# A third slot of prefix counts and 16 unread products a round in the edge sort of a graph network kernel

## The chip, the cores and the metric

The kernel runs on one core of a Trainium2 chip. The metric is the device time of one execution in microseconds (us), the median of several runs. Engines: TensorE (PE; its weight loads are PEld), VectorE (DVE), ScalarE (ACT), GpSimd (POOL) and SyncE (SP), each with its own in-order instruction stream; they meet by semaphores.

## What is computed

Four graph-network blocks run on one graph of 3125 nodes (48 features) and 100000 edges. Only the first step matters here: before any block can run, the edges are sorted on the chip. The reference, cut to what uses that order:

```
src, dst = edge_index[0], edge_index[1]
gate = silu(edge_attr @ F1W + F1b) @ F2W + F2b           # per edge, 48 wide
msg  = gate * h[dst] * (cw * mj)[:, None]
agg  = segment_sum(msg, src, num_segments=N)             # and softmaxes by src, by dst
```

Segment sums become products with 0/1 matrices if each record of an edge lies in the block of its source (25 blocks of 128 nodes) and the window of its destination (37 windows). So stage "bucket" gives every edge a rank among the edges of its block and window, computes the place from it, and scatters a 92-word record (attributes, gate, weights, source, destination) there in DRAM.

## The kernel before

The edges stand as 782 tiles of 128, and a set is SET = 16 tiles: NS = 49 sets, one for each round x of the stage. TensorE's and VectorE's loops run on to x = 55 and 56 to drain. A record travels through the rounds: `hh` (one-hot rows of window and block) for set x, prefix counts for x, same-cell counts for x - 1, ranks for x - 2, overflow for x - 4 and x - 5, gates for x - 6, places and records for x - 7. The order of the work on each engine is written out by hand; there is no planner.

TensorE, in round x, for each group g = 0 to 3 of four tiles (loop from line 403):

- `turn_hot(x, g)` (line 329): four transposes of `hh` into bank 0. It waits for `s_hot` and for ScalarE's copy of the group before.
- `cross(x, g)` (337, 340): accumulates, for all 17 prefixes of the set, the counts of window by block in partitions 0 to 36 of bank 1. At g = 0 it starts with the last prefix of the set before, read from `pre`, and waits for `s_pre`; at g = 3 it increments `s_cross`.
- `same(x - 1, g)` (350, 353): one 512-column product and four of 128 columns into bank 3.
- at g = 0 and 2 `mix(u)` (311), at g = 1 and 3 `gate(u)` (318), fp32, for the gates of eight tiles.
- at g = 1 `colds` (383, 384) and `spills` (371 to 375).
- after g = 3 `ahead(x - 2)` (361): 16 products of `hT` with `pre` into bank 2, `s_ahead`.

ScalarE copies the transposes to `hT` (440), turns the same-cell counts into `match` (447), and applies silu (433). VectorE, in round x: `one_hot(x + 1)`, `spill_ranks`, `places`, `before(x - 1)` (520: clips bank 1 into a slot of `pre`), two calls of `record` (509, 513: gate and words of eight tiles into `rec`), `pairs` (525), `ranks` (531 to 542). `before(s)` waits for `s_cross` and, as `pre` has two slots, for `ahead(s - 2)`:

```
dve.wait_ge(s_cross, s + 1)
if s >= 2:
    dve.wait_ge(s_ahead, s - 1)
```

GpSimd scatters: sixteen indirect DMAs a round (line 299), one for each tile, each four after a wait for `s_pos` and `s_rec`. The stage ends when they have landed. SyncE loads attributes; ahead of them it fills the lists in DRAM with empty records, and GpSimd waits for that before its first scatter.

Of the kernel before, what the change touches and what calls it, by code (L numbers as in the profile page):

```python
# [11 lines left out]
BF16 = mybir.dt.bfloat16  # L12
# [6 lines left out]
P = 128  # L19
N, E, H, RBF, LAYERS, G = 3125, 100000, 48, 40, 4, 32  # L20
NB = -(-N // P)
# [9 lines left out]
NW = len(WIN)  # L31
# [67 lines left out]
def bc(ap, n):  # L99

    return ap.unsqueeze(2).to_broadcast([ap.shape[0], ap.shape[1], n])
# [7 lines left out]
def along(ap, n):  # L109

    return ap.unsqueeze(1).to_broadcast([ap.shape[0], n, ap.shape[1]])
# [48 lines left out]
def bucket(nc, c, ps, m, a, w, given, list1, list2, wins, ncold, feats, nodes, embp, z, adapt, mult, logm, table0,  # L160
# [13 lines left out]
    SET = 16  # L174
# [4 lines left out]
    S1 = SET + 1  # L179
    HR, TR, MR, SR, LR = 5, 4, 4, 4, 10  # L180
# [2 lines left out]
    GATE, RECORD = 6, 7  # L183

    NAMES, TABLES = 3, NS + 2
    pad, pad2 = m.sb("pad", [P, 10, REC]), m.sb("pad2", [P, NW, 3])
    R = pad.shape[1]
    TIMES = HOT // P // R
# [5 lines left out]
    ge = m.sb("bk_ge", [P, SET, KT], BF16)  # L194
    hT = m.sb("bk_hT", [NW + NB, TR, SET * P], BF16)
    match = m.sb("bk_match", [P, MR, SET * P], BF16)
    pre = m.sb("bk_pre", [NW, 2, S1, NB], BF16)

    spill = m.sb("bk_spill", [P, SR, NB, SET], BF16)
    along_s = m.sb("bk_along", [P, SR, NB, SET], BF16)  # L200
# [8 lines left out]
    tri4 = m.sb("bk_tri4", [P, 4, P], BF16)  # L209
# [26 lines left out]
    with stage(nc, "bucket", *names, *[f"attr{k}" for k in range(4)], *[f"landed{k}" for k in range(RG)],  # L236
# [68 lines left out]
        @block.tensor  # L305
        def _(pe):
            def mix(u):
                pe.wait_ge(s_attr[u % 4], 16 * (u // 4 + 1))
                if u:
                    pe.wait_ge(s_silu, u)  # L310
                pe.matmul(ps[0:2 * H, 6, :], w["F1"][:], attrT[:, u % 4, :], start=True, stop=True).then_inc(s_mixed, 1)

            def gate(u):
                pe.wait_ge(s_silu, u + 1)
                if u >= 2:
                    pe.wait_ge(s_rec, 2 * (u - 1))
                for j in range(4):
                    ins = pe.matmul(ps[:, 5 + 2 * (u % 2), 2 * H * j:2 * H * j + 2 * H], hid[:, u % 2, P * j:P * j + P],  # L318
                                    w["F2"][:], start=True, stop=True)
                ins.then_inc(s_gated, 1)  # L320

            def turn_hot(s, g):
                x = 4 * s + g
                if g == 0:
                    pe.wait_ge(s_hot, s + 1)
                if x:
                    pe.wait_ge(s_flipped, x)
                for j in range(4):
                    ins = pe.transpose(flip[0:NW + NB, P * j:P * j + P], hh[:, s % HR, 4 * g + j, :], c["identb"][:])
                ins.then_inc(s_flip, 1)  # L330

            def cross(s, g):

                bank = ps[0:NW, 1, :]
                if g == 0:
                    pe.wait_ge(s_pre, s + 1)
                    pe.matmul(bank[:, 0:NB * S1], c["identb"][0:NW, 0:NW], along(pre[:, (s + 1) % 2, SET, :], S1), start=True,
                              stop=False)
                for t in range(4 * g, 4 * g + 4):
                    ins = pe.matmul(bank[:, NB * (t + 1):NB * S1], hh[:, s % HR, t, 0:NW], along(hh[:, s % HR, t, NW:], SET - t),  # L340
                                    start=False, stop=(t == SET - 1))
                if g == 3:
                    ins.then_inc(s_cross, 1)

            def same(s, g):
                x = 4 * s + g
                pe.wait_ge(s_flipped, x + 1)
                if x:
                    pe.wait_ge(s_match, x)
                pe.matmul(ps[:, 3, :], c["identb"][:], tri4[:].rearrange("p j e -> p (j e)"), start=True, stop=False)  # L350
                for j in range(4):
                    one = hT[:, s % TR, P * (4 * g + j):P * (4 * g + j) + P]
                    ins = pe.matmul(ps[:, 3, P * j:P * j + P], one, one, start=False, stop=(j == 3))
                ins.then_inc(s_same, 1)

            def ahead(s):
                pe.wait_ge(s_pre, s + 2)
                if s:
                    pe.wait_ge(s_rank, s)
                for t in range(SET):  # L360
                    ins = pe.matmul(ps[:, 2, NB * t:NB * t + NB], hT[0:NW, s % TR, P * t:P * t + P], pre[:, s % 2, t, :],  # L361
                                    start=True, stop=True)
                ins.then_inc(s_ahead, 1)

            def spills(s):
                pe.wait_ge(s_spill, s + 1)
                pe.wait_ge(s_srank, s + 1)
                if s > PLACE - SPILL - 1:
                    pe.wait_ge(s_pos, s - (PLACE - SPILL - 1))
                one, sums = spill[:, s % SR], along_s[:, s % SR]  # L370
                pe.matmul(ps[:, 4, 0:SET * NB], c["identb"][:], bc(carry_s[:], SET), start=True, stop=False)
                pe.matmul(ps[:, 4, SET * NB:S1 * NB], c["identb"][:], carry_s[:], start=False, stop=False)
                pe.matmul(ps[:, 4, 0:SET * NB], low[:], one.rearrange("p b t -> p (b t)"), start=False, stop=False)
                pe.matmul(ps[:, 4, 0:SET * NB], c["onesb"][:], sums.rearrange("p b t -> p (b t)"), start=False, stop=False)
                pe.matmul(ps[:, 4, SET * NB:S1 * NB], c["onesb"][:], sums[:, :, SET - 1], start=False, stop=True
                          ).then_inc(s_spilt, 1)

            def colds(s):
                pe.wait_ge(s_cold, s + 1)
                if s:  # L380
                    pe.wait_ge(s_pos, s)
                one = overb[:, s % LR, :]
                pe.matmul(ps[:, 4, 448:448 + SET], c["tri"][:], one, start=True, stop=True)
                pe.matmul(ps[:, 4, 480:480 + SET], c["onesb"][:], one, start=True, stop=True).then_inc(s_coldsum, 1)

            def turn_type(q):
                pe.wait_ge(s_emb, 16 * NB)
                if q:
                    pe.wait_ge(s_turned, q)
                for j, b in enumerate(by_four[q]):  # L390
                    ins = pe.transpose(ps[0:G, 5, P * j:P * j + P], embn[:, b, :], c["ident"][:])
                ins.then_inc(s_embT, 1)

            def adapted(q):
                pe.wait_ge(s_turned, q + 1)
                if q:
                    pe.wait_ge(s_named, q)
                for j, b in enumerate(by_four[q]):
                    ins = pe.matmul(ps[:, 7, G * j:G * j + G], embT[:, q % 2, P * j:P * j + P], adapt, start=True, stop=True)
                ins.then_inc(s_adapted, 1)  # L400
            pe.wait_ge(s_made, 4)
            pe.wait_ge(s_given, 16 * len(given))
            for x in range(NS + PLACE):
                for g in range(4):
                    if x < NS:
                        turn_hot(x, g)
                        cross(x, g)
                    if 0 <= x - 1 < NS:
                        same(x - 1, g)
                    if 0 <= 4 * (x - NAMES) + g < NQ:  # L410
                        turn_type(4 * (x - NAMES) + g)
                    if 0 < 4 * (x - NAMES) + g <= NQ:
                        adapted(4 * (x - NAMES) + g - 1)
                    if 0 <= x - GATE < NS:
                        u = 2 * (x - GATE) + g // 2
                        if g % 2 == 0:
                            mix(u)
                        else:
                            gate(u)
                    if g == 1 and 0 <= x - COLDS < NS:  # L420
                        colds(x - COLDS)
                    if g == 1 and 0 <= x - SPILL < NS:
                        spills(x - SPILL)
                if 0 <= x - AHEAD < NS:
                    ahead(x - AHEAD)
# [64 lines left out]
        def _(dve):  # L490
# [24 lines left out]

            def before(s):
                dve.wait_ge(s_cross, s + 1)
                if s >= 2:
                    dve.wait_ge(s_ahead, s - 1)
                dve.tensor_scalar(pre[:, s % 2].rearrange("p t b -> p (t b)"), ps[0:NW, 1, 0:NB * S1], 255.0, None, ALU.min  # L520
                                  ).then_inc(s_pre, 1)

            def pairs(s):
# [3062 lines left out]
```

## Time and profile before

| | us |
|---|---|
| median of 3 runs | 6147.38 (6138.8 to 6162.79) |
| span of the profiled execution | 6172.7 |
| TensorE busy, loads beside it | 4389.3 (71%) |
| VectorE busy | 3821.1 (62%) |
| GpSimd busy | 2684.3 (43%) |
| ScalarE busy | 2247.1 (36%) |
| line 299, 782 scatters of GpSimd | 790.6 busy, 529.6 idle before them |
| line 447, ScalarE's match | 134.7 busy, 408.2 idle before it |
| line 520, VectorE's `before` | 29.1 busy, 407.6 idle before it |

How to read it: the page gives shares over the whole span, but only the stage up to about 1370 us, where the last scatter stands, is touched. The idle time that stands before a line says who sits and waits; what ends that idle time is read from the waits and from the timeline of a single round. A matmul row shows when TensorE took the product and a modelled end; when others learn of the end is seen in the start of the row that waited. TensorE's granted clock is 1.0 (2.4 GHz) or 0.5 (1.2 GHz) at any time, and a mean over a stretch lies between.

### The profile page before, as it was taken

The numbers are of one execution on the slowest core, as the hardware profiler recorded it, in microseconds if no ns is written. First come the engines' busy times: TensorE is split into PE (matmuls) and PEld (weight loads), VectorE is DVE, ScalarE is ACT, GpSimd is POOL, SyncE is SP. The second block draws the span as 40 slices with busy tenths as digits, with TensorE's granted clock in tenths as the row PEclk, the third lists the DMA queues.
The fourth block names the chain that finished last, engine by engine and source line by source line (L and its number), as shares of the span: only waits on it lengthen the run. The fifth ranks groups of instructions, "written<-read, shape, count | busy, mean of one in ns | idle before, by whom it ended". The sixth has DMA issues, their size and how long they took to land. (4 is left out here: it accounts for less than half of the span.)

```text
span 6172.7 us, 186442 instructions
## 1 busy us (share of the span) xinstructions
PE 4389.3 (71%) x79347; PEld 3648.8 (59%) x79432; DVE 3821.1 (62%) x7925; ACT 2247.1 (36%) x7746; POOL 2684.3 (43%) x2702
## 2 busy tenths in 40 slices
PE   6676677725666479857985899489837765678887
PEld 3343344414555468846884788478835653677777
DVE  6555555538999767756774677477748335645244
ACT  3222222205666435543553455345520333300320
POOL 2666666666666346624662566256620340000000
PEclk7555555557999789968996999699959788788987
DMA  9222222227777344414331434144324626000000
GB/s 330 53 57 58 56 56 56 59 53 173 199 200 200 100 154 154 150 36 164 146 144 40 160 144 148 53 154 152 130 37 103 215 86 205 3 9 3 5 3 10
DMA packets 488183, 656.79 MB, mean 106 GB/s; under 512 B 316480, under 2 KB 370372, under 8 KB 484117
## 3 DMA queue, kind: packets, MB, share of 16 engines
q1 hardware_dynamic: 450965, 595.00, 30.7%
q0 software_dynamic: 33856, 48.44, 3.2%
q8 instruction: 644, 10.55, 0.7%
q14 instruction: 222, 1.82, 0.1%
q10 hardware_dynamic: 2496, 0.98, 0.1%
HBM read 464.16 MB, written 180.09 MB: 104 GB/s over the span
## 5 line engine op out<-in xcount | busy, mean ns | idle before, releaser
L299 POOL DMA_INDIRECT edges<-sb_bk_rec,sb_bk_pos x782 | 790.6, 1011 | 529.6 <-issue 224.1
L1681 ACT ACTIVATE sb_at_val<-banks,sb_at_prob 128x49 f32<-128x49 f32 x3800 | 773.5, 325 | 519.8 <-PE banks L1621 505.3
L1720 DVE TENSOR_REDUCE sb_at_tops<-banks 128x1 f32<-128x512 f32 x1000 | 626.0, 659 | 326.4 <-PE banks L1601 304.4
L1577 PE MATMUL banks<-sb_near,sb_at_hotT_d 128*128 128x49 bf16 x11100 | 618.8, 185 | 132.0 <-DMA sb_at_hotT_d<-rows_dst_t 65.5
L1535 POOL TENSOR_TENSOR sb_at_key<-sb_at_key,sb_at_attr 128x400 f32<-128x400 f32 (+1 forms) x400 | 371.0, 928 | 714.4 <-ACT sb_at_key L1665 622.1
L1577 PEld LDWEIGHTS banks<-sb_near,sb_at_hotT_d 128*128 128x128 fp8e4 x11100 | 567.1, 97 | 137.3 <-issue 70.7
L1579 PE MATMUL banks<-sb_queryp,sb_at_hotT_s 128*128 128x49 bf16 x11400 | 634.9, 186 | 16.4 <-issue 16.3
L1579 PEld LDWEIGHTS banks<-sb_queryp,sb_at_hotT_s 128*128 128x128 fp8e4 x11400 | 565.7, 96 | 18.9 <-issue 18.6
L1598 PE MATMUL banks<-sb_at_hotT_s,sb_off 128*128 128x512 fp8e4 x1000 | 374.4, 374 | 113.2 <-DVE sb_at_tops L1720 111.3
L1542 POOL TENSOR_TENSOR sb_at_val<-sb_at_val 128x490 f32<-128x490 f32 (+1 forms) x400 | 387.1, 968 | 67.7 <-ACT sb_at_val L1681 66.5
L1544 POOL TENSOR_TENSOR sb_at_val<-sb_at_val 128x490 f32<-128x490 f32 (+1 forms) x400 | 386.1, 965 | 31.3
L1621 PE MATMUL banks<-sb_near,sb_at_hotT_d 128*128 128x49 bf16 x11100 | 356.1, 186 | 32.4 <-ACT sb_at_val L1681 27.1
L1601 PE MATMUL banks<-sb_at_rows,sb_sel 114*128 114x128 bf16 x3800 | 374.5, 220 | 0.0
L1601 PEld LDWEIGHTS banks<-sb_at_rows,sb_sel 114*128 114x128 bf16 x3800 | 299.6, 98 | 113.9 <-issue 7.3
L1702 DVE TENSOR_TENSOR sb_at_key<-banks,sb_at_key 128x490 f32<-128x490 f32 (+1 forms) x400 | 254.1, 635 | 168.3 <-POOL sb_at_key L1535 168.2
L1621 PEld LDWEIGHTS banks<-sb_near,sb_at_hotT_d 128*128 128x128 fp8e4 x11100 | 330.0, 97 | 40.8 <-ACT sb_at_val L1681 34.6
L1632 PE MATMUL banks<-sb_at_val,sb_at_hot_s 128*128 128x147 bf16 x3800 | 338.9, 236 | 9.3 <-issue 5.4
L1665 ACT COPY sb_at_key<-banks 128x490 f32<-128x490 f32 (+1 forms) x400 | 231.0, 577 | 283.8 <-PE banks L1579 280.4
L1262 POOL TENSOR_TENSOR sb_gt_msg<-sb_gt_msg 128x245 f32<-128x245 f32 (+1 forms) x175 | 236.6, 1352 | 192.5 <-DVE sb_gt_msg L1409 191.6
L447 ACT ACTIVATE sb_bk_match<-banks,sb_bk_minus 128x512 bf16<-128x512 f32 x196 | 134.7, 687 | 408.2 <-remote 191.6
L520 DVE TENSOR_SCALAR sb_bk_pre<-banks 37x425 bf16<-37x425 f32 x49 | 29.1, 594 | 407.6 <-PE banks L361 355.3
L318 PE MATMUL banks<-sb_F,sb_bk_hid 97*128 97x96 f32 x784 | 191.0, 422 | 120.2 <-ACT sb_bk_hid L433 103.7
(690 smaller groups left out, 10689.2 us busy)
## 6 DMA issues: line engine op xcount, KB each, us to landing
sb_at_attr<-attr SPq DMA_DIRECT2D x100, 760.0 KB, 7.0
sb_at_hotT_s<-rows_src_t SPq DMA_DIRECT2D x100, 608.0 KB
sb_at_hot_s<-rows_src SPq DMA_DIRECT2D x100, 608.0 KB
sb_at_hotT_d<-rows_dst_t SPq DMA_DIRECT2D x100, 592.0 KB
edges<-sb_pad SPq DMA_DIRECT2D x95, 460.0 KB
sb_gt_rec<-edges SPq DMA_DIRECT2D x25, 1748.0 KB
sb_we_hotT<-rows_dst_t SPq DMA_DIRECT2D x52, 592.0 KB, 3.9
attr<-sb_gt_rec SPq DMA_DIRECT2D x25, 760.0 KB
```

Of the source, the lines that this page charges most:

```text
L299: pool.indirect_dma_start(list1, bass.IndirectOffsetOnAxis(pos[:, t:t + 1], 0), rec[:, k, j, :], None).then_inc(sent[k], 16)
L1535: pool.tensor_tensor(key[:, u % 2, 0:n, 0:RBF], key[:, u % 2, 0:n, 0:RBF], attr[:, i % 2, a:b, :], ALU.add).then_inc(s_key, 1)
L1542: pool.tensor_tensor(x[:, 0:n, 1, :], x[:, 0:n, 0, :], halves(0), ALU.subtract).then_inc(s_rest, 1)
L1544: pool.tensor_tensor(x[:, 0:n, 2, :], x[:, 0:n, 1, :], halves(1), ALU.subtract).then_inc(s_split2, 1)
L1577: pe.matmul(ps[:, 0, H1 * j:H1 * j + H1], where, what, start=(n == 0), stop=(n == 2))
L1579: ins = pe.matmul(ps[:, 1 + u % 2, H1 * j:H1 * j + H1], hotT_s[:, i % 4, k, :], queryp[:, i, n, :], start=(n == 0), stop=(n == 2))
L1598: pe.matmul(bank[:, 0:n], off[:], hotT_s[:, i % 4, ks[0]:ks[-1] + 1, :].rearrange("p k e -> p (k e)"), start=True, stop=False)
L1601: ins = pe.matmul(bank[:, P * j:P * j + P], sel[:, k, :], rows[:, i % 2, :], start=False, stop=(k == ks[-1]))
L1621: ins = pe.matmul(ps[:, 5, H1 * j:H1 * j + H1], where, what, start=(n == 0), stop=(n == 2))
L1632: ins = pe.matmul(ps[:, 6, 0:3 * H1], hot_s[:, i % 2, k, :], high(val[:, v % VB, j].rearrange("p n f -> p (n f)")), start=(k == 0), stop=( ...
L1681: ins = act.mul(val[:, v % VB, j, 0, :], ps[:, 5, H1 * j:H1 * j + H1], prob[:, i % 2, k:k + 1])
L1720: dve.tensor_reduce(tops[:, i % 2, g:g + 1], ps[:, 3 + x % 2, 0:P * len(RG[g])], AX, ALU.max).then_inc(s_top, 1)
```

## The change

TensorE gets a function `keep(n)`: n products of 512 columns, the first 64 columns of the bf16 identity as weights, `tri4` as data, into partitions 64 to 127 of bank 1, whose partitions 0 to 36 hold the counts. Nobody reads the result. `keep(4)` runs after the products of each group g, in all 56 rounds: 16 a round. `pre` gets three slots in place of two, and `before(s)` waits for `ahead(s - 3)` instead of `ahead(s - 2)`. Nothing else is changed.

```diff
@@ -183,6 +183,7 @@
     GATE, RECORD = 6, 7
 
     NAMES, TABLES = 3, NS + 2
+    SLOTS, KEEP = 3, 4
     pad, pad2 = m.sb("pad", [P, 10, REC]), m.sb("pad2", [P, NW, 3])
     R = pad.shape[1]
     TIMES = HOT // P // R
@@ -194,7 +195,7 @@
     ge = m.sb("bk_ge", [P, SET, KT], BF16)
     hT = m.sb("bk_hT", [NW + NB, TR, SET * P], BF16)
     match = m.sb("bk_match", [P, MR, SET * P], BF16)
-    pre = m.sb("bk_pre", [NW, 2, S1, NB], BF16)
+    pre = m.sb("bk_pre", [NW, SLOTS, S1, NB], BF16)
 
     spill = m.sb("bk_spill", [P, SR, NB, SET], BF16)
     along_s = m.sb("bk_along", [P, SR, NB, SET], BF16)
@@ -334,7 +335,7 @@
                 bank = ps[0:NW, 1, :]
                 if g == 0:
                     pe.wait_ge(s_pre, s + 1)
-                    pe.matmul(bank[:, 0:NB * S1], c["identb"][0:NW, 0:NW], along(pre[:, (s + 1) % 2, SET, :], S1), start=True,
+                    pe.matmul(bank[:, 0:NB * S1], c["identb"][0:NW, 0:NW], along(pre[:, (s + SLOTS - 1) % SLOTS, SET, :], S1), start=True,
                               stop=False)
                 for t in range(4 * g, 4 * g + 4):
                     ins = pe.matmul(bank[:, NB * (t + 1):NB * S1], hh[:, s % HR, t, 0:NW], along(hh[:, s % HR, t, NW:], SET - t),
@@ -358,7 +359,7 @@
                 if s:
                     pe.wait_ge(s_rank, s)
                 for t in range(SET):
-                    ins = pe.matmul(ps[:, 2, NB * t:NB * t + NB], hT[0:NW, s % TR, P * t:P * t + P], pre[:, s % 2, t, :],
+                    ins = pe.matmul(ps[:, 2, NB * t:NB * t + NB], hT[0:NW, s % TR, P * t:P * t + P], pre[:, s % SLOTS, t, :],
                                     start=True, stop=True)
                 ins.then_inc(s_ahead, 1)
 
@@ -382,6 +383,10 @@
                 one = overb[:, s % LR, :]
                 pe.matmul(ps[:, 4, 448:448 + SET], c["tri"][:], one, start=True, stop=True)
                 pe.matmul(ps[:, 4, 480:480 + SET], c["onesb"][:], one, start=True, stop=True).then_inc(s_coldsum, 1)
+
+            def keep(n):
+                for _ in range(n):
+                    pe.matmul(ps[64:P, 1, :], c["identb"][:, 0:64], tri4[:].rearrange("p j e -> p (j e)"), start=True, stop=True)
 
             def turn_type(q):
                 pe.wait_ge(s_emb, 16 * NB)
@@ -417,6 +422,7 @@
                             mix(u)
                         else:
                             gate(u)
+                    keep(KEEP)
                     if g == 1 and 0 <= x - COLDS < NS:
                         colds(x - COLDS)
                     if g == 1 and 0 <= x - SPILL < NS:
@@ -515,9 +521,9 @@
 
             def before(s):
                 dve.wait_ge(s_cross, s + 1)
-                if s >= 2:
-                    dve.wait_ge(s_ahead, s - 1)
-                dve.tensor_scalar(pre[:, s % 2].rearrange("p t b -> p (t b)"), ps[0:NW, 1, 0:NB * S1], 255.0, None, ALU.min
+                if s >= SLOTS:
+                    dve.wait_ge(s_ahead, s - SLOTS + 1)
+                dve.tensor_scalar(pre[:, s % SLOTS].rearrange("p t b -> p (t b)"), ps[0:NW, 1, 0:NB * S1], 255.0, None, ALU.min
                                   ).then_inc(s_pre, 1)
 
             def pairs(s):
```

## Rows read from the trace of the kernel before

**Rows 1.** Windows: busy us (x) of PE, PEld, DVE, ACT, POOL; clock, DMA share, GB/s

```profile
57.19:137.17 79.98, 74.40 (x508) 46.08 (x516) 53.55 (x99) 36.26 (x64) 0.00 (x0) 0.66 0.98 364
...
192.95:1206.47 1013.52, 727.55 (x3779) 413.38 (x3838) 574.75 (x1473) 250.47 (x400) 645.56 (x641) 0.55 0.23 56
```

**Rows 2.** Timeline of POOL, one round: start, us, engine, line, [idle before <- releaser]

```profile
598.13 0.96 POOL L299 DMA_INDIRECT edges<-sb_bk_rec,sb_bk_pos  x1 [4.53 <-DVE sb_bk_rec L513]
...
617.89 0.97 POOL L299 DMA_INDIRECT edges<-sb_bk_rec,sb_bk_pos  x1 [0.30 <-issue]
623.50 0.97 POOL L299 DMA_INDIRECT edges<-sb_bk_rec,sb_bk_pos  x1 [4.64 <-DVE sb_bk_rec L513]
```

**Rows 3.** Waits, 200 to 1200 us: who for whom, us in total, times, longest

```profile
DVE sb_bk_pre L520 <- PE banks L361: 324.6, 36, 9.8
ACT sb_bk_hT L440 <- remote: 185.6, 38, 5.8
...
POOL edges L299 <- DVE sb_bk_rec L513: 180.4, 39, 4.8
```

**Rows 4.** Timeline of PE, end of the same round

```profile
608.91 0.48 PE L353 MATMUL banks<-sb_bk_hT 62*128 62x128 bf16 x4
609.32 1.10 PE L311 MATMUL banks<-sb_bk_attrT,sb_F 80*96 80x512 f32 x2
610.35 0.41 PE L329 MATMUL banks<-sb_ident_bf,sb_bk_hh 128*62 128x128 bf16 x4
...
614.75 2.02 PE L318 MATMUL banks<-sb_F,sb_bk_hid 97*128 97x96 f32 x8 [0.93 <-ACT sb_bk_hid L433]
616.70 0.49 PE L361 MATMUL banks<-sb_bk_pre,sb_bk_hT 37*128 37x25 bf16 x12
618.27 0.18 PE L361 MATMUL banks<-sb_bk_pre,sb_bk_hT 37*128 37x25 bf16 x1 [1.07 <-issue]
619.70 0.18 PE L361 MATMUL banks<-sb_bk_pre,sb_bk_hT 37*128 37x25 bf16 x1 [1.26 <-issue]
621.10 0.20 PE L361 MATMUL banks<-sb_bk_pre,sb_bk_hT 37*128 37x25 bf16 x2 [1.22 <-ACT sb_bk_hT L440]
```

**Rows 5.** Timeline of ACT, the same stretch

```profile
611.87 0.69 ACT L447 ACTIVATE sb_bk_match<-banks,sb_bk_minus 128x512 bf16<-128x512 f32 x1 [3.36 <-remote]
...
620.40 0.58 ACT L440 COPY sb_bk_hT<-banks 62x512 bf16<-62x512 bf16 x1 [5.71 <-remote]
621.22 0.69 ACT L447 ACTIVATE sb_bk_match<-banks,sb_bk_minus 128x512 bf16<-128x512 f32 x1 [0.24 <-remote]
621.90 0.58 ACT L440 COPY sb_bk_hT<-banks 62x512 bf16<-62x512 bf16 x1
```

**Rows 6.** Timeline of a round before POOL's first scatter

```profile
125.05 0.39 PE L353 MATMUL banks<-sb_bk_hT 62*128 62x128 bf16 x4
...
125.48 0.69 ACT L447 ACTIVATE sb_bk_match<-banks,sb_bk_minus 128x512 bf16<-128x512 f32 x1 [0.42 <-PE banks L353]
```

**Rows 7.** Timeline of PEld, a weight load of line 361

```profile
618.99 0.10 PEld L361 LDWEIGHTS banks<-sb_bk_pre,sb_bk_hT 37*128 37x128 bf16 x1 [1.31 <-issue]
```

**Rows 8.** Timeline of PE: starts of products in a row, at both clocks

```profile
135.50 0.33 PE L374 MATMUL banks<-sb_bk_along,sb_ones_bf 128*128 128x400 bf16 x1
135.66 0.21 PE L375 MATMUL banks<-sb_bk_along,sb_ones_bf 128*128 128x25 bf16 x1
...
599.73 2.02 PE L311 MATMUL banks<-sb_bk_attrT,sb_F 80*96 80x512 f32 x2
...
606.76 0.54 PE L374 MATMUL banks<-sb_bk_along,sb_ones_bf 128*128 128x400 bf16 x1
607.09 0.23 PE L375 MATMUL banks<-sb_bk_along,sb_ones_bf 128*128 128x25 bf16 x1
```

**Rows 9.** Timeline of DVE around the end of the gap

```profile
621.58 0.59 DVE L520 TENSOR_SCALAR sb_bk_pre<-banks 37x425 bf16<-37x425 f32 x1 [9.01 <-PE banks L361]
622.09 0.54 DVE L509 TENSOR_TENSOR sb_bk_rec<-banks,sb_meta 128x384 f32<-128x384 f32 x1
```

## The prediction

> **What bounds the kernel now.** I first split the run with the windows view. Stage "bucket" (the sort) runs until GpSimd's last scatter at about 1370 us. TensorE is busy 728 of 1014 us in its middle part, at a granted clock of 0.55, which is nearly all at the lower level, 1.2 GHz [rows 1]. Nothing outside this stage is changed. The stage ends with POOL's 782 record scatters, so the question is what keeps POOL from scattering.
>
> POOL's timeline shows the period of the stage. Scatters start at 598.13, the sixteenth at 617.89, then POOL is idle for 4.64 us until 623.50 [rows 2]. So a round is 25.37 us: about 20.7 us of scatters back to back and a gap. Without the gap it would be 21.0 us. Over 200 to 1200 us POOL waited 180.4 us in 39 such gaps, all for VectorE's record copy [rows 3]. That copy stands behind `before(x-1)` in VectorE's order. VectorE itself is not the bound: `before` (line 520) waited 324.6 us for line 361, the products of `ahead` [rows 3].
>
> Why is TensorE late? The timelines of PE and ACT must be read side by side. The transposes of g = 3 are recorded at 610.35 and should be over by 610.76, but ScalarE's copy of them, which waits for nothing else new, starts only at 620.40. The products of line 353 of g = 2 are over at 609.39, the ACTIVATE that reads them starts at 611.87 [rows 4, 5]. In a round before the scatters begin the same step follows in 0.04 us (125.44 to 125.48) [rows 6]. So while POOL scatters, completions of TensorE reach the others late. The pace can be read from the weight loads and products of `ahead`, which need nothing, yet come singly: product 618.27, load 618.99, product 619.70, and with one load between the next product 621.10, so one instruction in 0.71 us [rows 4, 7]. Between the two late ACTIVATEs and the copy (611.87 and 620.40) lie 12 TensorE instructions (mix 2 + 2, transposes 4 + 4): 8.53 / 12 = 0.71 us again. About 1.5 to 2 us after POOL's last scatter the pace is gone: at 621.2 the rest comes out at once.
>
> The lateness begins, in this round, after about 98 instructions since POOL's restart at 598.13: by the code, the last of cross(0), same 5, mix 2, transposes 4, cross 4, same 5, gate 8, colds 2, spills 5, transposes 4, cross 4, same 5, that is 49 products (fp32 ones recorded twice), each with its weight load, in 11.3 us. I read it thus: **TensorE may complete some 95 instructions after POOL starts, then one in 0.71 us until POOL stops.** This is an inference from these rows; what stands behind it I don't know. It counts instructions, and the change adds instructions.
>
> **The change part by part.**
>
> `keep(4)`, four times a round: 16 products of 512 columns and 16 weight loads, so 32 more TensorE instructions on about 220 a round. Price of one: successive 400-column products start 0.33 us apart at the lower level (606.76 to 607.09) and 0.16 us at the upper (135.50 to 135.66) [rows 8]; scaled by 512/400 that is 0.42 and 0.21 us. Sixteen cost 6.8 or 3.4 us of TensorE a round. The weight loads hide behind the products. No `keep` waits and nobody waits for one, but TensorE is in order: queued behind are the next group's transposes (ScalarE waits), `colds` and `spills` (VectorE waits) and `ahead` (VectorE's ranks wait).
>
> The Trainium skill ("TensorE: Matmul & The Clock Gate", Part 1) says that the default clock is the halved one and sustained activity releases it. By that rule the additions would lift TensorE to 2.4 GHz, and its own work in a round would halve. I give that a rival below; the rows show the lower level in a stage with TensorE 72% busy, so I can't tell how much 16 products change it, and I take it part of the time.
>
> `before` writes three slots in turn and waits for ahead(s-3), not ahead(s-2). So it may run right after cross(x, 3), with same(3), gate, `keep` and `ahead` still queued. Now, cross(3), same(3), gate and `ahead` all complete within 0.4 us of each other when the jam clears: the g = 3 ACTIVATE, which needs same(3), follows the copy at 621.22, and `before` starts at 621.58 [rows 5, 9]. The gain is at most that 0.4 us a round, 17 us over 42 rounds; 0 at the other end. Its real use is to keep the `keep` and `ahead` of g = 3 out of the path.
>
> The slots' memory and memset (37 x 1275 for 37 x 850) cost under 0.4 us once. VectorE reading bank 1 beside TensorE writing other partitions of it is not in the trace: bounds 0 and one 0.42 us product a round (18 us in all); I take 0, as `before` has 0.59 us in every round now [rows 9]. No DMA or queue is moved.
>
> **The walk through one round after.** Time 0 is POOL's restart. It follows `before` by 1.92 us (621.58 to 623.50) [rows 2, 9], and TensorE has meanwhile gone on from cross(3) through same(3) to about the gate. The 95 instructions are now spent on: rest of gate 8, keep 8, `ahead` 32, transposes 8, cross(0) 10, same 10, mix 4, keep 8, and the transposes of g = 1. Before the change they reached g = 2. Then 0.71 us for each: until POOL's scatters are over and the jam clears at about 22.4 us (it cleared at 620.4 to 621.1, 22.3 to 23.0 after 598.13) some 20 more pass: cross(1) and same(1). The next 64 or so were handed to TensorE's queue meanwhile, as it is now (turn, cross, same, gate and 12 of `ahead`, 66, lie between the stuck transposes and the first single at 618.27), and come out at once. Left over before cross(3): mix(2), keep, transposes, cross(3). The pair of mix takes 2.02 us at the lower level and 1.10 at the upper [rows 4, 8]; the rest goes by columns, four transposes 512, cross(3) 250. At the lower clock: 2.0 + 1.7 + 0.4 + 0.2 = 4.3 us; at the upper 1.1 + 0.85 + 0.2 + 0.1 = 2.25 us. Then `before` and the way to POOL's restart, 1.9 us. Sum: 22.4 + 4.3 + 1.9 = 28.6 us, or 26.6 us at the upper clock. Against 25.37 that is +3.2 or +1.2 us a round. I take the middle, **+2.2 us**. Times 42 rounds (192.95 to 1206.47 has 40, and two more at the ends): +92 us. The first ten rounds lie under the list-filling DMAs that hold POOL until 137 us: 0. The seven rounds after the last sort round get 16 products each as well; for them I add one gap of the usual size, an estimate from [rows 2]: +5 us. Sum **+97 us**. The profiled span is 6172.7 us; with the change 6270 us by the same measure. The runs' median is 6147.4 us, 0.4% below the span, so I forecast 6147 + 97 = **6244 us**. Its own range is +1.2 to +4 us a round, 6195 to 6320 us.
>
> **The rivals.**
>
> Faster: the clock rises and the jam is one of time, not of count. Then each round reaches further before it. For it: TensorE's clock is at the lower level now, and its 18 us of work in a round (728 us for 40 rounds) [rows 1] would be 9 + 3.4 = 12.4 us with the additions at the upper. The floor is POOL's 21.0 us: 42 x 4.3 = 181 us, 5966 us. Half of that, 6057 us, is likelier since the jam would still come. It decides if TensorE completes cross(3) before POOL's sixteenth scatter. Against it: in the round shown TensorE was at the upper level from 609 to 612 (a pair of line 311 takes 1.10 us there, 2.02 at 599.73) and completions were late right then [rows 4, 5, 8]. Chance 0.23.
>
> No change: the added instructions fit into the jam (they pass while POOL scatters anyway) and the earlier `before` returns its 0.4 us: 6120 to 6175 us. It would also be so if the products don't lift the clock and the queue hides them. For it: TensorE idles or trickles for some 10 us a round. Against: that time is one of 14 completions, not of work. Chance 0.14.
>
> Much slower: the clock stays at the lower level, the additions are 6.8 us of work and the queue hides little; left over after the jam is everything from gate(1) on: gate 2.0 (614.75) [rows 4], keep 1.7, spills 1.1, transposes 0.4, cross(2) 0.5, same(2) 0.9 by their columns, and the 4.3 above, 10.9 us, of which I let half hide: 22.4 + 5.4 + 1.9 = 29.7 us a round, +4.3, so 181 + 5 us in all, 6333 us. For it: clock 0.55 now. Chance 0.13.
>
> **How the numbers follow.** Forecast 0.50, much slower 0.13, faster 0.23, no change 0.14. A measurement of this kernel tells some 0.5% (31 us) from no change. Faster 0.23, same 0.14, slower 0.63. The range leaves out about a tenth on each side: the stronger half of the faster rival below 6060 us, and the upper end of the much slower one, where less than half hides, above 6360 us.
>
> **What the profile would show.** Right: POOL's period at 26.5 to 29 us, its gap at 6 us or more; ACT's late copy moved from g = 3 to g = 1 or 2; `before` starts ahead of the `ahead` products; granted clock in the stage above 0.6. Wrong: a gap under 4 us, or late completions at the same place as before. The forecast falls if the lateness doesn't count instructions, or if the added products take no part in it.

## The result and the profile after

| | before | changed |
|---|---|---|
| median | 6143.09 us (6134.46 to 6162.79) | 6227.01 us (6219.17 to 6234.86) |
| ratio, 95% interval | 1 | 1.0133 [1.0118, 1.0148] |
| span of the profiled execution | 6172.7 us | 6217.5 us |

The change costs 84 us by the medians (of four runs each; the table ahead of the prediction has three of the four). The profiled execution of before was 30 us above its median and that of after 10 us below, so the two spans differ by only 45 us. The last scatter, which ends the stage, moved from 1369.5 to 1421.4 us, +52 us; what follows it took 4803 us before and 4796 us after. So the profiles show where 52 us of the loss arise; the other 32 us of the 84 can't be placed by these two traces. The line numbers have moved: line 299 is now 300, 520 is 526, 513 is 519, 440 is 446, 447 is 453, 548 is 554, 353 is 354, 361 is 362, 375 is 376, 318 is 319; the added products are line 389.

The windows of after, to set beside [rows 1] (busy us (x) of PE, PEld, DVE, ACT, POOL; clock, DMA share, GB/s):

```profile
192.95:1206.47 1013.52, 810.55 (x4219) 399.95 (x4218) 549.57 (x1387) 234.78 (x379) 609.17 (x602) 0.65 0.21 53
```

TensorE is busier (811 for 728 us) at a higher granted clock (0.65 for 0.55), and GpSimd got fewer scatters done in the same time, 602 for 641. The waits of after, 200 to 1200 us (who for whom, us in total, times, longest), beside [rows 3]:

```profile
ACT sb_bk_hT L446 <- remote: 317.7, 61, 9.3
POOL edges L300 <- DVE sb_bk_rec L519: 224.5, 36, 9.8
DVE sb_bk_tmp L554 <- remote: 188.2, 19, 13.3
...
DVE sb_bk_pre L526 <- remote: 106.6, 20, 9.2
```

GpSimd waits for the record 44 us longer in total, in 36 waits for 39. VectorE's wait ahead of the prefix counts fell from 325 us [rows 3] (353 us with three waits marked "remote", of which the profile names no engine) to 107 us, but a new one of 188 us in 19 times stands at line 554, the first instruction of `spill_ranks`, which takes TensorE's product of line 376 (with the 12 waits that the profile puts down to that line, 241.5 us in 31 times). The timeline of POOL, first scatters after a gap (start, us, line, [idle before]), beside [rows 2]:

```profile
569.05 0.97 POOL L300 DMA_INDIRECT edges<-sb_bk_rec,sb_bk_pos  x1 [9.44 <-DVE sb_bk_rec L519]
593.95 0.97 POOL L300 DMA_INDIRECT edges<-sb_bk_rec,sb_bk_pos  x1 [4.18 <-DVE sb_bk_rec L519]
623.98 0.97 POOL L300 DMA_INDIRECT edges<-sb_bk_rec,sb_bk_pos  x1 [9.49 <-DVE sb_bk_rec L519]
648.94 0.97 POOL L300 DMA_INDIRECT edges<-sb_bk_rec,sb_bk_pos  x1 [4.23 <-DVE sb_bk_rec L519]
```

Here is the loss. Rounds are of two kinds: 25.0 us with a gap of 4.2 us, a little shorter than before, and 30.0 us with a gap of 9.5 us. Of the 45 gaps after the first scatter (waits of over a microsecond) 16 are over 7 us; before, 3 of 43 were, one in start-up and two in the drain. From the restart of set 2 to that of set 42 both kernels run 40 rounds. Before they take 25.34 us in the mean and none is long; after, 16 are long (29.97 us in the mean) and 24 short (24.97), and the mean is 26.97 us. That is 65 us more in the 40 rounds. The start-up is 8.5 us shorter (set 2 starts at 184.43 for 192.95 us) and the drain 5 us shorter, which leaves the 52 us.

**What makes a long round.** The round from 593.95 to 623.98, first ScalarE, then TensorE, then VectorE:

```profile
599.55 0.58 ACT L446 COPY sb_bk_hT<-banks 62x512 bf16<-62x512 bf16 x1 [6.00 <-remote]
...
611.73 0.69 ACT L453 ACTIVATE sb_bk_match<-banks,sb_bk_minus 128x512 bf16<-128x512 f32 x1 [4.38 <-remote]
616.89 0.58 ACT L446 COPY sb_bk_hT<-banks 62x512 bf16<-62x512 bf16 x1 [4.48 <-remote]
```

```profile
596.89 0.63 PE L330 MATMUL banks<-sb_ident_bf,sb_bk_hh 128*62 128x128 bf16 x4
...
604.67 0.60 PE L354 MATMUL banks<-sb_bk_hT 62*128 62x128 bf16 x4
...
610.06 0.23 PE L376 MATMUL banks<-sb_bk_along,sb_ones_bf 128*128 128x25 bf16 x1
610.22 0.59 PE L330 MATMUL banks<-sb_ident_bf,sb_bk_hh 128*62 128x128 bf16 x4
...
617.96 0.42 PE L341 MATMUL banks<-sb_bk_hh 128*37 128x100 bf16 x4
...
623.18 0.60 PE L362 MATMUL banks<-sb_bk_pre,sb_bk_hT 37*128 37x25 bf16 x16
```

```profile
604.00 0.79 DVE L508 TENSOR_REDUCE sb_bk_win<-sb_bk_ge 128x16 f32<-128x608 bf16 x1
616.91 0.87 DVE L554 TENSOR_TENSOR sb_bk_tmp<-banks,sb_bk_spill 128x400 f32<-128x400 f32 x1 [12.12 <-remote]
...
621.85 0.17 DVE L587 CAST sb_bk_pos<-sb_bk_place 128x16 uint32<-128x16 f32 x1
622.06 0.59 DVE L526 TENSOR_SCALAR sb_bk_pre<-banks 37x425 bf16<-37x425 f32 x1
```

The transposes of 596.89 end at 597.52 and are copied at 599.55, 2.0 us late; those of 610.22 should be over by 610.8 and are copied at 616.89, 6.1 us late, 22.9 us after GpSimd's restart. At that moment, with POOL's sixteenth scatter some 2 us past, the jam clears. The last product of `spills`, recorded at 610.06, is released then too, and VectorE, idle for 12.12 us, only now begins `spill_ranks` and `places`: 20 small instructions, 616.91 to 622.06, 5.15 us, that stand ahead of `before` in its order. TensorE's rest (`cross(3)` at 617.96) is done beside them and costs nothing. In the kernel before the same chain ran ahead of the jam's worst part:

```profile
607.43 0.87 DVE L548 TENSOR_TENSOR sb_bk_tmp<-banks,sb_bk_spill 128x400 f32<-128x400 f32 x1 [0.82 <-issue]
...
612.39 0.17 DVE L581 CAST sb_bk_pos<-sb_bk_place 128x16 uint32<-128x16 f32 x1
```

So after the change the jam begins earlier in the round, `spills` falls into it, and 5.15 us of VectorE's work move from under the scatters to behind them. It holds for every round and not only for this one: in all 16 long rounds line 554 starts 21.4 to 23.3 us after the restart and `before` 5.15 to 5.63 us after it; in the 24 short ones line 554 starts by 18.75 us, and the gap is at most 4.75 us. After a long round the next one is a short one in this trace, but for one; presumably TensorE, with 9.5 us without jam, has then got ahead (on chip B below two long ones often stand in a row). Why the jam begins earlier no row shows.

The third slot works as written: `before` at 622.06 stands ahead of the `ahead` products at 623.18.

### The profile page after: what moved, and what is told of

The parts are those of the page before. It is cut to its first block and busy times, and to the rows that moved or that the text cites. A ratio compares the mean times of both kernels' runs of the same rounds, so it can differ in the third digit from the quotient of the medians.

```text
span 6217.5 us, 188319 instructions
## 1 busy us (share of the span) xinstructions
PE 4543.8 (73%) x80328; PEld 3651.6 (59%) x80328; DVE 3831.3 (62%) x7925; ACT 2252.9 (36%) x7746; POOL 2688.1 (43%) x2702
## 5 line engine op out<-in xcount | busy, mean ns | idle before, releaser
L389 PE MATMUL banks<-sb_bk_tri,sb_ident_bf 128*64 128x512 bf16 x896 | 341.5, 519 | 7.1 <-issue 6.7
L446 ACT COPY sb_bk_hT<-banks 62x512 bf16<-62x512 bf16 x196 | 113.4, 579 | 589.8 <-remote 387.5
L1638 PEld LDWEIGHTS banks<-sb_at_val,sb_at_hot_s 128*128 128x128 fp8e4 x3800 | 267.4, 100 | 11.5 <-issue 6.4
```

The source lines that it names most:

```text
L1638: ins = pe.matmul(ps[:, 6, 0:3 * H1], hot_s[:, i % 2, k, :], high(val[:, v % VB, j].rearrange("p n f -> p (n f)")), start=(k == 0), stop=( ...
```

## The experiments

Two theories. **Count:** completions are late while GpSimd scatters, by the number of instructions, so 16 added products hurt whatever their width. **Work:** the products hurt by TensorE's time that they take, 0.42 or 0.21 us each. These runs were on four chips, called A to D in order of use; which chip the first comparison had isn't recorded. Each ratio is against the kernel before on the same chip. Those of keep_narrow_2 and keep_only_2 rest on two runs of the changed kernel.

| run | chip | slots, products a group | us | before | ratio |
|---|---|---|---|---|---|
| slots_only | A | 3, 0 | 5913.25 | 5915.96 | 0.9997 [0.9985, 1.0009] |
| keep_only | A | 2, 4 | 5917.99 | 5915.96 | 1.0006 [0.9993, 1.0019] |
| keep_narrow | A | 3, 4 of 64 columns | 5913.15 | 5915.96 | 1.0002 [0.9990, 1.0014] |
| keep_one | A | 3, 1 | 5908.79 | 5915.96 | 0.9989 [0.9979, 0.9999] |
| before_again | B | 2, 0 | 6151.85 | 6168.86 | one run |
| after_again | B | 3, 4 | 6282.65 | 6168.86 | 1.0183 [1.0159, 1.0207] |
| keep_narrow_2 | C | 3, 4 of 64 columns | 6243.28 | 6154.30 | 1.0152 [1.0099, 1.0204] |
| keep_one_2 | C | 3, 1 | 6138.85 | 6154.30 | 0.9968 [0.9952, 0.9985] |
| slots_only_2 | C | 3, 0 | 6146.86 | 6154.30 | 1.0001 [0.9983, 1.0019] |
| keep_only_2 | D | 2, 4 | 6324.50 | 6147.89 | 1.0279 [1.0234, 1.0323] |
| no_scatter | D | 2, 0 | 5741.26 | 6147.89 | one run |
| pause8b | D | 2, 0 | 6176.46 | 6147.89 | one run |

### Each part alone, and a cheap or a single product

```diff
slots_only:   SLOTS, KEEP = 3, 0
keep_only:    SLOTS, KEEP = 2, 4
keep_one:     SLOTS, KEEP = 3, 1
keep_narrow:  (with 3, 4)
-                    pe.matmul(ps[64:P, 1, :], c["identb"][:, 0:64], tri4[:].rearrange("p j e -> p (j e)"), start=True, stop=True)
+                    pe.matmul(ps[64:P, 1, 0:64], c["identb"][:, 0:64], tri4[:, 0, 0:64], start=True, stop=True)
```

> Three slots of prefix counts, no added products. Count theory (TensorE may complete some 95 instructions after POOL's first scatter of a round, then one in 0.71 us until POOL stops): the earlier `before` lets POOL restart earlier as seen from TensorE, so `ahead` and the next transposes fall into the counted stretch; rounds get no shorter and may turn uneven, mean 25.4 to 26.7 us, total 6140 to 6200 us. Rival (the wait on ahead is worth what it looks like, 0.4 us a round): 6120 to 6135 us, rounds of 25.0 us.

> Sixteen added products a round, two slots. Count theory: rounds of 27.3 to 29.7 us, total 6220 to 6320 us, at least as long as the changed kernel, since `before` now also waits for the keep and ahead of g = 3. Rival (the slots do the harm, the added products none): 6130 to 6160 us.

> The changed kernel with the added products cut from 512 to 64 columns: as many instructions, an eighth of the columns (under 1 us of TensorE a round for 6.8 at the lower clock). Count theory: most of the loss stays, 6190 to 6225 us, more than with one product of 512 columns in each group. Work theory (the 3.4 to 6.8 us of columns cost the time): 6130 to 6155 us, less than with one product of 512 columns.

> The changed kernel with one product of 512 columns in each group for four: a quarter of the instructions (8 a round) and of the columns (1.7 us a round at the lower clock, against under 1 us of the narrow ones). Count theory: 6150 to 6190 us, less than the narrow kernel by 20 us or more. Work theory: a quarter of the loss, 6150 to 6175 us, and more than the narrow kernel.

**Measured:** all four within 0.12% of the kernel before, which on chip A takes 5916 us, some 230 us less than on the chip of the first comparison. The windows and ScalarE beside TensorE in slots_only, then its waits of POOL from 200 to 1200 us:

```profile
192.95:1206.47 1013.52, 652.47 (x3851) 362.77 (x3850) 645.36 (x1636) 249.09 (x400) 750.66 (x748) 0.62 0.28 67
```

```profile
610.74 0.63 PE L330 MATMUL banks<-sb_ident_bf,sb_bk_hh 128*62 128x128 bf16 x4
```

```profile
611.41 0.58 ACT L446 COPY sb_bk_hT<-banks 62x512 bf16<-62x512 bf16 x1 [2.36 <-PE banks L330]
```

```profile
POOL edges L300 <- issue: 220.3, 722, 0.3
...
POOL edges L300 <- DVE sb_bk_rec L519: 3.4, 11, 0.3
```

The copy follows its transposes (over at 611.37) in 0.04 us in the middle of GpSimd's scatters: on this chip there are no late completions. GpSimd does 739 scatters in the window (the 748 count nine instructions of the next stage) and waits 3.4 us for VectorE; it is the bound, its last scatter stands at 1158.2 us, and what TensorE does between makes no difference. None of the four expectations, all made for a stage with late completions, came true, and none could be tested here. What the runs do show: the products themselves, their slots and their bank cost nothing where TensorE has slack.

### The changed kernel and the kernel before once more

No edit. The question was whether the first comparison's loss belonged to a chip with late completions.

> The changed kernel once more, beside the kernel before on the same chip. In the four kernels run so far no completion of TensorE came late, POOL scattered without gaps of over 2.2 us and the kernel before took 5916 us there against 6143 in the first comparison. Theory: the loss of the first comparison needs the late completions; where they are missing POOL is the bound (782 scatters of 1.3 us) and the changed kernel takes 5900 to 5930 us, equal to the kernel before within 0.3%. Rival (the loss belongs to the change as such): 5980 to 6010 us beside 5916. If the late completions are there: 6210 to 6240 beside 6130 to 6160.

> The kernel before, for its profile on this chip. Theory: if it takes about 5916 us, ScalarE's copies follow TensorE's transposes in 0.04 us all through the sort, POOL's last scatter stands at about 1160 us instead of 1370, and the sort rounds are over by about 870 us. Rival (the time differs elsewhere): late completions as before and the last scatter at 1370 us.

**Measured** on chip B: 6282.65 us, +1.83%; the kernel before had one run of 6151.85 us with its profile. Its pattern is that of the first chip, gaps of 4.5 to 4.8 us, last scatter at 1370.2 us: the rival of before_again is right, and 6282.65 us is above the 6210 to 6240 us expected of the changed kernel. In the changed kernel 24 of 45 gaps are over 7 us, and the last scatter stands at 1480.6 us. All gaps after the first scatter add up to 328 us, against 218 us in before_again; the 110 us between them are the shift of the last scatter. The waits of VectorE (200 to 1200 us):

```profile
DVE sb_bk_tmp L554 <- remote: 272.1, 26, 14.0
```

The loss follows the number of rounds in which line 554 is caught: 19 such waits and +84 us on the first chip, 26 and +114 us here. Of the 40 rounds 22 are long, in all of them line 554 starts later than 21 us after the restart, and in none of the 18 others. The mean round is 28.07 us against 25.37.

### The same variants where completions are late

> The changed kernel with the added products cut from 512 to 64 columns, for a chip that shows the late completions (there the kernel before takes 6130 to 6180 us; where they are missing, 5916 us, nothing changes). Count theory: 32 instructions a round are still added, so most of the loss stays: 1.0% to 1.8% slower than the kernel before, and slower than with one product of 512 columns. Work theory: under 0.4% slower, and less than with one product of 512 columns.

> The changed kernel with one product of 512 columns in each group, for a chip with the late completions. Count theory: a quarter of the added instructions, 0.2% to 1.0% slower than the kernel before and less than the narrow kernel. Work theory: 1.7 us of columns a round at the lower clock against under 1 us, so slower than the narrow kernel.

> Three slots, no added products, for a chip with the late completions. Count theory: POOL restarts earlier as seen from TensorE, so `ahead` falls into the counted stretch: 0 to 1.0% slower than the kernel before, rounds uneven. Rival (the wait on ahead is worth 0.4 us a round): 0.2% to 0.4% faster, rounds of 25.0 us.

**Measured** on chip C. keep_narrow_2, windows and waits:

```profile
192.95:1206.47 1013.52, 689.97 (x4100) 403.16 (x4172) 545.13 (x1375) 226.82 (x372) 605.32 (x601) 0.55 0.21 53
```

```profile
DVE sb_bk_tmp L554 <- remote: 230.7, 24, 14.0
```

The narrow products take an eighth of the columns, TensorE's work is nearly that of before the change (690 us in 601/16 rounds, 18.4 us a round, for 18.2), the clock is the old 0.55, and the loss is the same within the noise: +1.52%, 601 scatters in the window as after the full change (602), gaps of 9.4 us again, 16 long rounds of 40. **The cost is in the instructions, a product and its weight load each, not in their time.**

With one product a group (four a round) the gaps are short for the most part (8 of 43 over 7 us, 5 long rounds of 40) and the median shows no loss; it is even 0.3% below that of before, where the count theory expected 0.2% to 1.0% more. I can't explain that and leave it open. The profiled execution does show a cost beside the slots alone on the same chip: 0, 8 and 32 added instructions a round (slots_only_2, keep_one_2, keep_narrow_2) make 0, 5 and 16 long rounds of 40, and the last scatter stands at 1355.1, 1377.7 and 1442.9 us. These are single executions, that of keep_one_2 the slowest of its eight. With the slots alone:

```profile
618.71 0.97 POOL L300 DMA_INDIRECT edges<-sb_bk_rec,sb_bk_pos  x1 [4.29 <-DVE sb_bk_rec L519]
643.63 0.97 POOL L300 DMA_INDIRECT edges<-sb_bk_rec,sb_bk_pos  x1 [4.16 <-DVE sb_bk_rec L519]
```

The round is 24.92 us, against 25.37 in [rows 2] (in the mean of 40 rounds 24.96 against 25.34), even and not uneven as the count theory had it, and the last scatter stands at 1355.1 us, 14 to 15 us earlier than in the two profiles of before, on the first chip and on B. In the medians (1.0001 [0.9983, 1.0019]) a gain of that size, 0.24%, isn't seen; the interval's lower end, 0.17%, is a little short of it.

### Sixteen products with two slots

The edit is that of keep_only, on chip D.

> The 16 products a round with two slots of prefix counts, now wanted on a chip that shows late completions. Then VectorE's count waits for the products of line 361 again, which come behind the last four added products and are 32 completions more. Theory of the count: it loses at least what the whole change loses, 1.3 to 3% over the kernel before, since the third slot is what keeps the last group's additions out of the path. If the third slot were without use, it would lose the same as the whole change, 1.3 to 1.8%. Theory of the work (columns, not instructions, cost): about 1 to 2% as well, so this run tells only what the slot is worth. On a chip without late completions: no difference (0.1%), as in the first such run.

**Measured:** +2.79%, 177 us: 1.5 to 2 times the changed kernel's loss. Nearly every gap is now long (37 of 43 over 7 us). TensorE, VectorE and the waits:

```profile
628.71 2.02 PE L319 MATMUL banks<-sb_F,sb_bk_hid 97*128 97x96 f32 x8 [1.65 <-ACT sb_bk_hid L439]
630.66 1.92 PE L389 MATMUL banks<-sb_bk_tri,sb_ident_bf 128*64 128x512 bf16 x4
632.51 0.60 PE L362 MATMUL banks<-sb_bk_pre,sb_bk_hT 37*128 37x25 bf16 x16
```

```profile
633.25 0.59 DVE L526 TENSOR_SCALAR sb_bk_pre<-banks 37x425 bf16<-37x425 f32 x1 [12.68 <-PE banks L362]
```

```profile
DVE sb_bk_pre L526 <- PE banks L362: 389.5, 34, 12.7
```

GpSimd restarted at 604.94, the jam cleared at 628, again 23 us later. With two slots `before` must wait for `ahead`, and gate (2.02), the four added products (1.92) and `ahead` (0.60) come after the jam one behind the other, at the lower clock: 4.5 us in the open. That is a second way to the same gap of 9.5 us, and the third slot removes it. Line 554 isn't caught here: in all 40 rounds it starts within 11.7 us of the restart. The 60 to 90 us between this run and the changed kernel are from different chips, so their size is rough.

### Does the lateness come from the scatters?

```diff
no_scatter:
-                    if t < TILES:
-                        pool.indirect_dma_start(list1, bass.IndirectOffsetOnAxis(pos[:, t:t + 1], 0), rec[:, k, j, :],
-                                                None).then_inc(sent[k], 16)
...
pause8b:
+                    if (t + 1) % 8 == 0:
+                        for _ in range(8):
+                            busy(pool.memset(idle[:], 0.0))
```

In no_scatter SyncE waits for `s_rec` in place of the scatters' semaphore.

> The kernel before without the 782 scatters: it leaves out the placing of the records in the lists, so all that follows works on empty lists. Everything else of the stage runs. Theory: the lateness of TensorE's completions comes with the scatters. Without them ScalarE's ACTIVATE of line 447's group follows its product within 0.1 us all through the stage, and a sort round takes TensorE's work of 15 to 19 us instead of 25.4: VectorE's last count of prefixes (at about 1204 us in the kernel before) comes at 750 to 950 us. Rival (the lateness belongs to TensorE's own stream of work, to its instructions or its clock, and not to the scatters): sort rounds keep over 23 us and the last count comes after 1100 us.

> The kernel before, with GpSimd made to pause after each eight scatters (eight linked memsets of a 128x128 scratch tile, 97 pauses; I estimate 2 to 7 us each from nothing better than the gap of 4.3 us in which TensorE's completions came through). Theory of the count: the lateness of TensorE is cleared whenever GpSimd stops scattering, so with a pause in mid-round few completions are late, VectorE's record is there before GpSimd wants it, and the waits of GpSimd for VectorE's record (180 us in 39 times between 200 and 1200 us in the kernel before) fall below 60 us. The pauses themselves are then the cost: last scatter at 137 + 782 x 1.27 + 97 pauses, 1370 to 1700 us. Rival (completions are late for as long as the stage lasts, whether GpSimd scatters at that moment or not): the waits for the record stay at 150 us or more on top of the pauses. On a chip that shows no late completions even in the kernel before it tells nothing but the price of a pause.

**Measured** on chip D. In no_scatter the prefix counts of VectorE (duration ns, first and last start) and three of them in a row:

```profile
L515 DVE TENSOR_SCALAR sb_bk_pre<-banks x49: 592/595/598, 32.2 to 870.2; 37x425 bf16<-37x425 f32 x49
```

```profile
613.16 0.59 DVE L515 TENSOR_SCALAR sb_bk_pre<-banks 37x425 bf16<-37x425 f32 x1 [3.38 <-PE banks L356]
629.80 0.59 DVE L515 TENSOR_SCALAR sb_bk_pre<-banks 37x425 bf16<-37x425 f32 x1 [0.29 <-PE banks L356]
645.38 0.59 DVE L515 TENSOR_SCALAR sb_bk_pre<-banks 37x425 bf16<-37x425 f32 x1
```

Rounds of 15.6 to 16.6 us here, of 19.7 elsewhere, and the last set at 870 us instead of 1204: as forecast, but for the 19.7, which is above the 15 to 19 us expected. ScalarE follows at once:

```profile
606.13 0.60 PE L348 MATMUL banks<-sb_bk_hT 62*128 62x128 bf16 x4
```

```profile
606.77 0.69 ACT L442 ACTIVATE sb_bk_match<-banks,sb_bk_minus 128x512 bf16<-128x512 f32 x1 [1.04 <-PE banks L348]
```

On the same chip the kernel keep_only_2 had the late completions, so the rival, that TensorE's own stream makes them, falls: they come with the scatters. Whether it is GpSimd's issuing, the writes or their semaphore increments isn't separated. The total of 5741 us says no more, since all later stages work on empty lists.

In pause8b no wait of GpSimd for the record is left among its waits from 200 to 1200 us, where before it was 180.4 us [rows 3]:

```profile
POOL edges L301 <- issue: 168.6, 550, 1.2
POOL edges L301 <- POOL sb_bk_idle L306: 42.1, 78, 0.6
```

A pause costs 2.3 us (2.06 of memsets and the step to the next scatter), 97 of them some 223 us, as much as the 218 us of gaps that they replace: the last scatter stands at 1376.4 us, the run at 6176 us. The last set's counts come at 1025.5 us, 179 us earlier than before, so two pauses of 2.3 us a round let TensorE pass as well as one gap of 4.6 us or better. ScalarE's copy still waited 243.7 us for late completions: 2.3 us clear the jam only in part. A shorter pause might win what the gaps cost; it wasn't tried. It is one run.

## Why the prediction was right, and where not

Forecast 6244 us, +97; measured 6227 us, +84. By its steps:

- **The bound and the place of the loss: right.** GpSimd waits for the record behind `before`; the last scatter ends the stage. What the profiles show of the loss is in the gaps: GpSimd's waits for the record went from 218.0 to 268.0 us over the stage, the last scatter by 52 us.
- **"TensorE may complete some 95 instructions after POOL starts, then one in 0.71 us until POOL stops": half right.** The scatters cause it (no_scatter), it counts instructions (keep_narrow_2), and it clears about 23 us after the restart (22.9 in after, 23 in keep_only_2; I had 22.3 to 23.0). But the two numbers are no constants. In after the first completion is late at 5.6 us after the restart (599.55), where I had 11.3 us and 98 instructions; some 26 products with their loads lie between. (The round has about 190 instructions by [rows 1], not 220.) And in keep_only_2 ScalarE's copy at 616.58 and its ACTIVATE at 625.11 are 8.53 us apart with nine products and their loads between, 0.47 us each.
- **"Left over before cross(3): 4.3 or 2.25 us": the step that failed.** The walk put on the path what TensorE had left. It named VectorE as one who waits for `spills` but gave that wait no price. In the trace it is the whole price: 5.15 us of `spill_ranks` and `places` in 16 rounds of 40 (22 on chip B), and TensorE's rest hidden behind them. The evenly longer round of 26.6 to 28.6 us doesn't exist; there are rounds of 25.0 and of 30.0 us, and the sign "a gap of 6 us or more" holds in 16 of 40 only. The mean round grew by 1.6 us in the first comparison and by 2.7 us on chip B, and the forecast had +2.2. That this fits is luck: the two prices are of one size, and the share of rounds that pay was not in the sum. The timelines show this path in all 59 long rounds of after, after_again, keep_narrow_2 and keep_one_2; no run took VectorE's chain out of it.
- **Late copy moved from g = 3 to an earlier group: right,** to g = 2 (the transposes of 610.22 stand right behind `spills`, the end of g = 1).
- **Slots at most 0.4 us a round: right** (mean round 25.34 to 24.96). Their use with the products, to keep `keep` and `ahead` of g = 3 out of the path, was named but not priced: keep_only_2 shows it as 2.02 + 1.92 + 0.60 us a round.
- **Price of a product 0.42 us at the lower clock, and bank 1 shared at no cost: right.** Line 389 starts every 0.42 to 0.43 us (602.28, 602.71, 603.14), and `before` takes 595 ns still. By keep_narrow_2 neither matters.
- **Start-up 0 and drain rounds +5 us: wrong,** both got shorter. From the last `before` to the last scatter it was 165 us and is 160 us (1261.4 to 1421.4), and set 2 starts 8.5 us earlier.
- **The clock: it rose, above 0.6 as said, and gave nothing.** The granted clock went from 0.55 to 0.65 with 512-column products and stayed at 0.55 with 64-column ones; on chip A it was 0.62 with slots alone and 0.73 with the 16 products of 512 columns (keep_only). The rule of the Trainium skill ("TensorE: Matmul & The Clock Gate", Part 1), that sustained activity releases the halved clock, agrees with the direction. The rival built on it fell because the round's length isn't TensorE's work: from 611 to 617 us, at a mean granted clock of 0.75, it was held up by completions, and TensorE was busy 3.9 of the 6 us.

## What to carry to other kernels

Before adding idle-filling instructions to an engine, ask who waits for its completions, how much work each waiter has behind that wait, and whether these run under something long; price the waiter's chain, not the added instructions. Where completions are late, a change's cost can be in the count of instructions: here an eighth of the columns cost the same. And when a mean comes out as forecast, look at the single rounds: here two kinds stood behind it. And look first whether the chip at hand shows the bottleneck at all: on one of them this change was free.

## What of the hardware was not expected

- **Chips differ in kind.** On chip A TensorE's completions reached ScalarE in 0.04 us while GpSimd scattered, and the kernel before, which has no profile there, took 5916 us; on the first chip and on B, C and D it took 6143 to 6169 us, and every trace taken there of a kernel with its scatters shows late completions, by up to some 10 us (9.6 us in [rows 4, 5]). What differs between the chips no run shows. One difference stands in the traces themselves: those of chip A hold some 41000 records of semaphore increments by DMAs, those of the other chips, taken with the scatters, 26000 to 29000, and only chip A's give the scatters' time from issue to landing, a median of 2.2 to 2.3 us. So elsewhere such records are in part missing, and a releaser called "remote" or "issue" is uncertain there. Whether missing and late have one cause is open.
- **A 64-column product is as dear as a 512-column one** in this stage (+1.5% for sixteen a round), while four of 512 columns show no loss in the median (0.9968 [0.9952, 0.9985]). In the profiles the number of long rounds grows with the added instructions: 0, 5 and 16 of 40 for 0, 8 and 32 a round.
- **The lateness is no fixed rate.** 0.71 us an instruction in the round of [rows 4], 0.47 us in keep_only_2; that it ends about 23 us after the restart, some 2 us after the sixteenth scatter, was the same in three kernels.
